# Order of TensorE's work in attention, and the layout of two scratch tensors, in a gated cross-attention block

## The reference

```
x = x + tanh(g_xattn) * xattn(layernorm(x), ctx, ctx)   # rotary positions on q and k, ALiBi bias, softmax
x = x + tanh(g_ffn)   * ffn(layernorm(x))

ffn:  x    = act_qdq(x)                     # 16 bits, one scale: max|x| of the whole tensor
      up   = act_qdq(x @ w_up.T)            # weights in 4 bits by blocks of 32
      gate = act_qdq(x @ w_gate.T)
      sig  = round(sigmoid(gate) * 65536) / 65536
      gate = act_qdq(gate * sig)
      o    = act_qdq(gate * up)             # 1536 columns
      return o @ w_down.T
```

## Time and profile before

| | us |
|---|---|
| median of three runs (1800.41 to 1803.16) | 1801.39 |
| profiled execution | 1800.73 |
| its span, first to last instruction | 1798.9 |
| granted TensorE clock, mean over the span | 0.965 of full speed |
| PE matmul, line 934 (scores): busy, count | 365.9, x4096 |
| PE matmul, line 921 (maxima): busy, count | 334.7, x4096 |
| PE matmul, line 983 (P.V): busy, count | 265.5, x2048 |
| DVE reduction, line 1348: busy, count | 600.3, x512 |
| ACT exponential, line 1145: busy, count | 556.8, x1024 |
| POOL sum, line 1936: busy, count | 441.0, x93 |

### The profile page before, as it was taken

The page is one execution under the profiler, slowest core; times in us unless marked ns, Lnnn a source line. Parts: engine busy times, 40 slices in busy tenths (PEclk is TensorE's granted clock), DMA queues, the critical chain, the costliest instruction groups (busy, mean ns, idle before and its releaser), DMA issues. The chain is left out here.

```text
span 1798.9 us, 36886 instructions
## 1 busy us (share of the span) xinstructions
PE 1605.8 (89%) x14777; PEld 633.3 (35%) x14777; DVE 1479.7 (82%) x2116; ACT 1241.8 (69%) x1974; POOL 838.6 (47%) x504
## 2 busy tenths in 40 slices
PE   3899999999999999999869999999999900699999
PEld 0233333333333333333224444444444400344444
DVE  7899999999998898898569989768889998854551
ACT  3688888888889899888723323359986699844440
POOL 5699999999999999998600100200000000000000
PEclk9999999999999999999979999999999955899999
DMA  6688888988888887776649888569973479755551
GB/s 153 151 154 179 167 164 180 177 164 167 163 173 161 171 183 151 163 151 136 139 117 275 242 250 239 203 194 284 280 226 127 139 250 302 237 189 172 176 168 61
DMA packets 344204, 331.73 MB, mean 184 GB/s; under 512 B 214849, under 2 KB 273601, under 8 KB 336097
## 3 DMA queue, kind: packets, MB, share of 16 engines
q1 hardware_dynamic: 335104, 264.37, 55.2%
q0 software_dynamic: 8928, 65.02, 18.3%
HBM read 136.77 MB, written 76.55 MB: 119 GB/s over the span
## 5 line engine op out<-in xcount | busy, mean ns | idle before, releaser
L1348 DVE TENSOR_REDUCE cm<-quad 128x1 f16<-128x1024 f32 x512 | 600.3, 1214 | 63.3 <-PE quad L921 62.3
L1145 ACT ACTIVATE P<-quad 128x512 f32<-128x512 f32 x1024 | 556.8, 598 | 112.3 <-PE quad L934 100.5
L1936 POOL TENSOR_TENSOR Ps<-P,P 128x2048 f32<-128x2048 f32 x93 | 441.0, 4742 | 43.2 <-ACT P L1145 43.1
L934 PE MATMUL quad<-QA,KA 101*32 101x512 f16 x4096 | 365.9, 385 | 6.8 <-ACT P L1145 5.3
L921 PE MATMUL quad<-KA,QA 100*32 100x512 f16 x4096 | 334.7, 391 | 35.6 <-DMA QA<-S 17.8
L983 PE MATMUL quad<-P,cg 128*32 128x512 f32 x2048 | 265.5, 594 | 0.0
L1010 PE MATMUL quad<-x_hl,Wu 128*128 128x512 f16 x1152 | 250.8, 381 | 3.4 <-DMA Wu<-wt_scratch 3.4
L1010 PE MATMUL quad<-x_hl,Wg 128*128 128x512 f16 x1152 | 249.3, 379 | 3.1 <-DMA x_hl<-xs 2.5
L1063 PE MATMUL quad<-Wd,oh 128*128 128x512 f16 x768 | 228.6, 379 | 0.0
L934 PEld LDWEIGHTS quad<-QA,KA 101*32 101x32 f16 x4096 | 105.0, 94 | 298.6 <-ACT P L1145 231.0
L1226 ACT ACTIVATE ev<-quad 128x1024 f32<-128x1024 f32 x96 | 97.3, 1014 | 123.4 <-PE quad L1010 117.3
(11 more groups left out here) (167 smaller groups left out, 2006.3 us busy)
## 6 DMA issues: line engine op xcount, KB each, us to landing
Ps<-P POOLq DMA_DIRECT2D x62, 1024.0 KB, 8.1
gate_scratch<-ev SPq DMA_DIRECT2D x48, 512.0 KB, 3.8
gt<-gate_scratch SPq DMA_DIRECT2D x48, 512.0 KB, 5.8
up_scratch<-ev SPq DMA_DIRECT2D x48, 512.0 KB, 3.4
uf<-up_scratch SPq DMA_DIRECT2D x48, 512.0 KB, 5.1
uf<-up_scratch SPq DMA_DIRECT2D x96, 256.0 KB, 3.6
wt_scratch<-wh SPq DMA_DIRECT2D x72, 128.0 KB, 2.8
xl<-in_x_dram SPq DMA_DIRECT2D x32, 256.0 KB, 5.1
```

What stands on the lines that cost most here:

```text
L934: mm = e.matmul(K.score[h % 2][j:j + 32, :], K.KA[p % 2][0:101, kt, h, j:j + 32], K.QA[p % 2][0:101, 4 * qc:4 * qc + 4, h, :], start=True, ...
L1145: e.activation(K.Pb[pb][:, h, :], K.score[h % 2], ACT.Exp, scale=SCALE / (QPOW * KPOW)).then_inc(K.a_exp, 1)
L1348: e.tensor_reduce(cm[:, col:col + 1], K.quad[UNIT["max", hm, u] % 2][:, :], AX.X, ALU.max).then_inc(K.v_max, 1)
L1936: e.tensor_tensor(K.Ps[n][:, :, :], K.Pb[(st.g - 1) % NP][:, :, :], K.Pb[st.g % NP][:, :, :], ALU.add).then_inc(K.g_sum, 1)
```

## The change

Two edits.

In the tensor program the order in a step becomes: score 0, maxima, score 1, maxima, P.V of the step before, score 2, maxima, score 3, maxima. In step 1 P.V stays behind the denominators at the end. P.V moves into a function `numerators`; what each instruction waits for and computes is the same. Steps without maxima keep the order of the rest.

The scratch tensors for gate and up get the shape (ot, cp, 128, 1024) in place of (ot, 128, 4096): a tile of 128 x 1024 lies in one piece of 512 KB. Stores and loads address it so; their number, their sizes and their places in SP's order don't change.

```diff
-        self.gate_d = nc.dram_tensor("gate_scratch", (OT, 128, N), F32).ap()
-        self.up_d = nc.dram_tensor("up_scratch", (OT, 128, N), F32).ap()
+        self.gate_d = nc.dram_tensor("gate_scratch", (OT, N // GW, 128, GW), F32).ap()
+        self.up_d = nc.dram_tensor("up_scratch", (OT, N // GW, 128, GW), F32).ap()
...
-        e.dma_start(dst_d[ot, :, 1024 * cp:1024 * cp + 1024], K.ev[k % NEV][:, :]).then_inc(K.d_ev[k % NEV], 16)
+        e.dma_start(dst_d[ot, cp, :, :], K.ev[k % NEV][:, :]).then_inc(K.d_ev[k % NEV], 16)
...
-        e.dma_start(K.gt[n % NGT][:, :], K.gate_d[ot, :, GW * cp:GW * cp + GW]).then_inc(K.d_gt[n % NGT], 16)
+        e.dma_start(K.gt[n % NGT][:, :], K.gate_d[ot, cp, :, :]).then_inc(K.d_gt[n % NGT], 16)
...
-        e.dma_start(K.uf[n % NUF][:, 0:w], K.up_d[ot, :, sl]).then_inc(K.d_uf[n % NUF], 16)
+        e.dma_start(K.uf[n % NUF][:, 0:w], K.up_d[ot, cp, :, sl]).then_inc(K.d_uf[n % NUF], 16)
...
+    def numerators(before):
+        if before is None or not before.inside:
+            return
+        hf, kt, p = before.hf, before.s, before.p
+        if kt == 0 and hf > 0:
+            e.wait_ge(K.a_num, hf)
+        e.wait_ge(K.a_exp, score_no(hf, kt, 3))
+        for h in range(4):
+            mm = e.matmul(K.num[32 * h:32 * h + 32, :], K.cg[(p + 1) % 4][:, kt, 32 * h:32 * h + 32],
+                          K.Pb[before.g % NP][:, h, :], start=kt == 0, stop=kt == 7)
+        mm.then_inc(K.pe_pv, 1)
+
     before = None
     for st in STEPS:
         if st.inside:
             score(st.hf, st.s, 0)
+        if st.maxima:
+            row_max(st.hm, 2 * st.im, 0)
+        if st.inside:
             score(st.hf, st.s, 1)
         if st.maxima:
-            row_max(st.hm, 2 * st.im, 0)
             row_max(st.hm, 2 * st.im, 1)
-            row_max(st.hm, 2 * st.im + 1, 0)
+        if st.s != 1:
+            numerators(before)
         if st.inside:
             score(st.hf, st.s, 2)
         if st.maxima:
-            row_max(st.hm, 2 * st.im + 1, 1)
+            row_max(st.hm, 2 * st.im + 1, 0)
         if st.inside:
             score(st.hf, st.s, 3)
-
-        if st.s == 1 and st.dens is not None:
-            denominators(*st.dens)
-        if before is not None and before.inside:
...
+        if st.maxima:
+            row_max(st.hm, 2 * st.im + 1, 1)
+        if st.s == 1:
+            if st.dens is not None:
+                denominators(*st.dens)
+            numerators(before)
```

More of the change, by code:

```diff
@@ L847, in sync_program, with load_up @@
     uf_uses = [0]
-    def load_up(ot, sl, w):
+    def load_up(ot, cp, sl, w):
         n = uf_uses[0]
@@ L856, in load_up @@
                 e.wait_ge(K.a_uq, n - NUF - 48 + 1)
-        e.dma_start(K.uf[n % NUF][:, 0:w], K.up_d[ot, :, sl]).then_inc(K.d_uf[n % NUF], 16)
+        e.dma_start(K.uf[n % NUF][:, 0:w], K.up_d[ot, cp, :, sl]).then_inc(K.d_uf[n % NUF], 16)
     def load_product(n):
-        load_up(n // 4, slice(GW * (n % 4), GW * (n % 4) + GW), GW)
+        load_up(n // 4, n % 4, slice(0, GW), GW)
     def load_o(n):
         ch, ot = TODO[n]
-        load_up(ot, slice(512 * ch, 512 * ch + 512), 512)
+        load_up(ot, ch // 2, slice(512 * (ch % 2), 512 * (ch % 2) + 512), 512)
     def load_xr(n):
```

## The result

| | before | after |
|---|---|---|
| median of four runs, us | 1801.99 | 1829.09 |
| range, us | 1800.41 to 1803.16 | 1828.46 to 1829.82 |
| span of the profiled execution, us | 1798.9 | 1828.0 |

The changed kernel is slower: ratio 1.0151, 95% interval 1.0134 to 1.0169, +27 us. Forecast was +20 (1821).

The account below looks back on a forecast made before the run. Attention was taken to have three engines (TensorE, VectorE, GpSimd) within a few per cent of full. 21 halves at +0.83 us and ten at +0.4 gave +21; last steps 0, layout -1: 1800.7 to 1821 us, range 1782 to 1838.

Parts of the forecast that it names:

- ScalarE's loop: Attention, two score banks: 1.09 us from score start to bank release; plain steps 2.82 us instead of 2.68, +0.28 a half.
- late second unit: Attention steps: the second unit of maxima ends with the step, its reduction starting no earlier than 2.8 us in.
- end of attention: Last ten steps, without maxima: up to -6 us on TensorE, counted as 0 because TensorE waits for VectorE's last sum.
- its own signs: Included a half near 27.3 us in the first stretch, and gt and uf landing within 0.3 us of before.
- Step 7: s = 7 of a half: first maxima held by the reduction, new wait 0.65 us; taken as +0.40 (0 to +0.5).
- Steps 3 and 4: s = 3: +0.14 from ScalarE; late second units of s = 2 and 4 holding next first maxima: +0.15 together.
- Step 0: s = 0 of a half: wait of 0.43 us goes, 0.14 comes, about 0.1 behind the statistics; -0.15.
- Step 6: s = 6 of a half in attention: forecast as nothing, 0.
- the ten halves where GpSimd never rested: Second stretch of attention: part of the longer chain hides in waits on GpSimd, taken as +0.4 us a half.
- The layout's term: Gate and up scratch, pitch 16 KB to 4 KB: taken as -1 us, bounds -8 and +5.
- Rival (a): Attention: VectorE sets the pace and even spacing wins, 1783 us; sign: s = 7's first maxima within 0.3 us; chance 0.20.
- Rival (b): Attention: GpSimd and VectorE set the pace whatever TensorE's order, halves stay 26.5 to 26.9 us, 1800 us; chance 0.13.

Follow-up runs that it names:

- pv_before_s3: Kernel before, old scratch layout, with P.V moved one place earlier, before score 3 (step 1 unchanged): 1876.17 us, ratio 1.0420.
- half reductions: VectorE's reduction of a unit of maxima reads 512 of its 1024 columns, old layout: 1784.72 us with the old order, 1801.33 us with the new.
- padding: Kernel before with 1024 unused columns added to gate and up scratch, rows of a tile 20 KB apart instead of 16 KB: 1791.60 us, ratio 0.9948.
- before_halfmax: Kernel before, but VectorE's reduction of a unit of maxima reads only the last 512 of 1024 columns: 1784.72 us, ratio 0.9920.
- cols13: New layout, alternating scores and maxima, P.V cut by queries: columns 0 to 127 mid-step, 128 to 511 at the end; against kernel before 1788.27 us, ratio 0.9933.
- alt_vlast: Old layout, scores and maxima alternate as in the changed kernel, P.V stays at the step's end; against kernel before 1809.41 us, ratio 1.0042.
- split13: New layout, alternating order, one head of P.V mid-step and three at the end, step 1 as before; against kernel before 1829.76 us, ratio 1.0159.
- order_only: Kernel before with only the new order of TensorE's work, old scratch layout: 1839.68 us against 1799.31, ratio 1.0223.

## Why the prediction was right, and where it was not

Right, and shown: the direction; ScalarE's loop as the rule of the order (1.09 us from a score to its bank, in four kernels of different order; 2.82 forecast and 2.83 seen for a plain step, though the means of steps 0 and 5 are 2.89; `pv_before_s3` in its range); the late second unit (ready at 2.84, 2.8 forecast) with step 7's first maxima as the place where it tells (0.70 of wait, 0.65 worked out), taken away by half reductions; the end of attention, which gave back none of what the order lost. Of its own signs two failed: a half is 27.98 us in the first stretch and not near 27.3, and gt and uf land 0.4 and 0.7 us sooner and not within 0.3 of before.

That the total is as near as +27 to +20 is in part luck, for two errors cancel: the order was put at +21 and costs +37 to +40; the layout was put at -1 and gives -7 to -9.

In the order's sum the terms that were mis-sized are these. Step 7 was worked out at +0.5 and then taken at +0.40; it measured +0.64. Steps 3 and 4 were given 0.14 and 0.15 together; they measured +0.61. Step 3's first maxima wait 0.40 us every other half, 0.2 on average, for step 2's late second unit, where the text allowed 0.1 at most. The transposes of step 4 start 0.39 us late where 0.11 stood, for they wait for the first unit's reduction (VectorE's row statistics come just ahead of it, behind the late unit), which was named nowhere in the text. Step 0 gained 0.08 and not 0.15: the waits for the second unit were read from single steps (0.43 at step 0, 0.30 at step 7), and their means are 0.33 and 0.17. Step 6 gained 0.23 unforecast: the denominators come later in it, and no longer wait for the accumulated sum. And the ten halves where GpSimd never rested were counted at +0.4, for a part of the loss was to hide behind it; they lost 0.91, and the others in the first stretch 1.45 and not 0.83. A chain just under GpSimd's 26.8 us that grows by more than 1 us passes it; the overlap could hide only the first tenths.

The layout's term was read from rows that don't show it. The half tiles of the earlier trace rows (3.7 us before) land in 4.1 in the same stretch of the changed kernel, with rows 4 KB apart, and the down projection takes 248.4 to 248.6 us in every kernel of the study. So most of the 2.9 against 3.7 is not the pitch (over the span half tiles land in 3.6 us before, in 3.4 with padding). What counts are the whole tiles (5.1 to 4.4). And "TensorE runs unbroken through nearly all of the first" passed over the 3.4 us that it waits for `Wu` there and the stretch at half clock behind the second wait; these are 5.4 of the 9 us. The page of the kernel before has these waits in its row of these matmuls: 3.4 us idle, ended by `Wu`.

Rival (a) rested on VectorE's 94%. Its own sign decides against it: step 7's first maxima come 0.92 us into the step and not within 0.3. And half reductions show that VectorE's waits were mostly a place to wait for GpSimd. Rival (b) was half right, as a floor to gains (26.8 to 26.9 us in the second stretch in before, `before_halfmax` and `cols13`) and not to losses.

Open: why half 0 differs by 1 to 2.5 us from one execution to the next; how much of `cols13`'s 4 us over the layout is its own; why half tiles land in 3.4 us with padding but in 3.9 with rows 4 KB apart.

## What to carry to other kernels

Before moving a block of TensorE's work, measure from one plain stretch how long an engine takes to give a bank back, and write beside each pair of uses of a bank the work that lies between them: a block that makes one gap larger takes it from another. Where several engines are within a few per cent of full, removing a wait moves it to the next of them, and a new wait costs only what doesn't fall where one stood (1.8 us of new waits made a half of `alt_vlast` 0.35 us longer); a nearly full engine hides losses only up to its slack. Read the mean of a wait over all halves before it goes into a sum. Cut work that is spread over column strips along what the strips have in common (here the queries): one strip's part holds up what follows as long as the whole. And look at everything behind a transfer in its queue: here faster tile loads paid most by letting weight loads start sooner.

## What was not expected of the hardware

- One head of P.V holds its strip for 0.86 us (472.94 to 473.80 in `split13`), the four heads in four strips take 0.86 together. Of the group of four matmuls behind it three start with head 0's second record (473.36) and the fourth 0.44 us later, though the program has it first; ScalarE is released by the fourth (474.24).
- After a wait of 2.45 us for a load TensorE's granted clock is 0.50, the lower of its two levels, for 3.4 us (kernel before, 1333.9); behind a wait of 2.37 us in `order_only` (1373.5) it stays at 1.00.
- P.V as 16 records of 128 and 384 columns takes 0.22 and 0.64 us, together no more than 8 of 512.
- GpSimd's sums take the same time beside a VectorE that is 30% less busy: 424.50 and 424.55 us of work in the first stretch.
- Tiles whose rows of 4 KB lie 16 KB apart land about 10% later than with 20 KB (5.1 against 4.6 us for 512 KB).
